# Attention and FFN kernel: two score chunks ahead of the transposes in steps 0 and 1, no clearing of y, bias first in a batch's first steps, the last block transfers issued by two engines

## What is computed

```python
x = L0_attn_x                          # (2, 1024, 512), float32
xn = _layernorm(x, axis=-1)
s = _L0_attn_ref(xn, ...)
g = _silu(_L0_ffn_ref(xn, ...))
x = x + s * g
```

## Time and profile before

| | us |
|---|---|
| median of 3 runs | 2310.16 |
| the runs | 2310.16, 2304.26, 2310.84 |
| the profiled execution, whole | 2305.63 |
| its span from first to last instruction | 2303.8 |
| busy: PE, DVE, ACT, POOL | 2193.3, 1806.7, 1330.2, 792.2 |
| mean granted TensorE clock | 0.989 of full speed |

### The profile page before, as it was taken

One profiled execution on the slowest core, in us unless ns is written; L12 is line 12 of the kernel. 1 busy time (PEld: TensorE's weight loads), 2 busy tenths in 40 slices (PEclk: granted clock), 3 DMA queues, 4 the chain that ended last, 5 costly groups with the idle time before them and its releaser, 6 DMA issues.

```text
span 2303.8 us, 37079 instructions
## 1 busy us (share of the span) xinstructions
PE 2193.3 (95%) x10928; PEld 1845.2 (80%) x10928; DVE 1806.7 (78%) x3917; ACT 1330.2 (58%) x3700; POOL 792.2 (34%) x2053
## 2 busy tenths in 40 slices
PE   5999999999999999799989999999999999998998
PEld 5888888888888888588877888878888878876887
DVE  5889899999989989723369898989898989896132
ACT  3666666666666666433356666666666666654333
POOL 1424242424242424144514242424242424221443
PEclk8999999999999999999999999999999999999999
DMA  2454556454545454623325555555545555445223
GB/s 97 128 122 122 128 123 126 126 127 125 124 123 128 124 127 123 164 83 133 119 77 127 126 125 127 123 124 126 128 122 127 124 128 122 101 122 137 96 96 110
DMA packets 432682, 278.93 MB, mean 121 GB/s; under 512 B 55520, under 2 KB 416096, under 8 KB 428512
## 3 DMA queue, kind: packets, MB, share of 16 engines
q1 hardware_dynamic: 432480, 276.56, 48.0%
HBM read 119.12 MB, written 6.29 MB: 54 GB/s over the span
## 4 chain that ended last, share of the span: by engine, by line
PE 85%; DVE 5%; issue 4%; SPq 2%; POOL 2%; ACT 2%; DMA 1%; DVEq 0%; ACTq 0%; POOLq 0%
PE out_ps L425 17%; PE out_ps L437 14%; PE score_ps L411 10%; PE even_ps L388 7%; PE qkv_ps L388 6%; PE third_ps L411 5%; PE score_ps L499 5%; PE qkv_ps L499 5%; PE even_ps L389 3%; PE qkv_ps L389 3%; PE even_ps L515 3%; SPq L306 2%; DVE probs L831 1%; PE third_ps L515 1%; PE out_ps L515 1%
## 5 line engine op out<-in xcount | busy, mean ns | idle before, releaser
L845 DVE TENSOR_TENSOR pT_lo<-pT_lo,pT_hi 128x512 fp32r<-128x512 f32 x576 | 380.1, 704 | 95.1 <-ACT pT_hi L595 95.0
L587 ACT ACTIVATE probs<-probs,low_min 128x896 f32<-128x896 f32 (+7 forms) x512 | 394.9, 780 | 97.4 <-DVE low_min L820 95.6
L595 ACT ACTIVATE pT_hi<-pT_lo 128x512 fp32r<-128x512 f32 x576 | 330.7, 622 | 173.5 <-PE out_ps L425 119.9
L831 DVE STREAM_TRANSPOSE probs<-probs 128x896 f32<-128x896 f32 (+7 forms) x512 | 373.9, 753 | 0.7
L1045 POOL TENSOR_SCALAR rs_x<-sq_sum 128x5 f32<-128x5 f32 x122 | 33.6, 275 | 901.2 <-ACT natural L563 898.6
L425 PE MATMUL out_ps<-pT_hi,kv_hi 128*128 128x512 f32 x576 | 236.6, 411 | 50.0 <-issue 45.8
L600 ACT ACTIVATE attT_hi<-att 128x512 fp32r<-128x512 f32 x128 | 81.0, 632 | 328.6 <-DVE att L852 328.6
L425 PE MATMUL out_ps<-pT_hi,kv_lo 128*128 128x512 f32 x576 | 225.9, 392 | 0.0
L425 PE MATMUL out_ps<-pT_lo,kv_hi 128*128 128x512 f32 x576 | 225.5, 392 | 0.0
L437 PE MATMUL out_ps<-o_hi,attT_hi 128*128 128x512 f32 x512 | 213.1, 416 | 9.3 <-DVE attT_lo L859 9.3
L820 DVE CUSTOM_DVE_ANT_0 probs<-score_ps,rel_sb,slope 128x384 f32<-128x384 f32 (+5 forms) x352 | 203.7, 589 | 1.9 <-PE score_ps L411 1.1
(11 more groups left out here) (203 smaller groups left out, 6052.1 us busy)
## 6 DMA issues: line engine op xcount, KB each, us to landing
qkv_raw<-w_ffn_dram SPq DMA_DIRECT2D x44, 768.0 KB, 4.3
att<-rec_out_at SPq DMA_DIRECT2D x128, 256.0 KB, 5.1
pT_lo<-probs SPq DMA_DIRECT2D x256, 128.0 KB, 3.6
pT_lo<-probs SPq DMA_DIRECT2D x256, 112.0 KB, 3.6
pT_lo<-probs SPq DMA_DIRECT2D x256, 96.0 KB, 3.1
qkv_raw<-w_qkv_dram SPq DMA_DIRECT2D x15, 1536.0 KB, 6.5
pT_lo<-probs SPq DMA_DIRECT2D x256, 80.0 KB, 2.6
o_raw<-w_o_dram SPq DMA_DIRECT2D x16, 1024.0 KB, 5.5
```

The costliest lines, as they stand in the source:

```text
L587: act.activation(row, row, ACT.Exp, scale=-1.0, bias=low_min[:, i % 2, h, HEAD_CHUNKS[i] - 1:HEAD_CHUNKS[i]], accum_out=row_sum[:, i % 2, ...
L595: act.activation(pT_hi[:, (U * TURNS + n) % HIGH_SLOTS, :], home(i, j).bitcast(F32), ACT.Copy).then_inc(probs_high, 1)
L831: dve.transpose(row, row).then_inc(probs_turned, 1)
L845: dve.tensor_tensor(out=home(i, j), in0=home(i, j).bitcast(F32), in1=pT_hi[:, (U * TURNS + n) % HIGH_SLOTS, :].bitcast(F32), op=ALU.subtra ...
```

## The change

It does four things; the matmuls and the transfers are the same.

1. `parts_of` returns `SBANKS - (i < LAG)` for `between`: in steps 0 and 1 of every unit but a batch's first, two chunks of `scores` (and two `bias`) stand between `project` and `turn_qk`, not three. The third follows `out_project` (on VectorE `add_y`). These are 14 units with two such steps each.
2. The clearing of `y` is gone with its semaphore. In the second unit of a batch steps 0 to 2 copy into `y` in place of adding.
3. In steps 0 and 1 of a batch's first unit VectorE runs all four `bias` before `low_q` and `low_k`. In step 0 `early_norms` of the third tile moves from before the `bias` to behind `low_k`; in the first batch the two `low_x` of that step move ahead of `low_q`.
4. In the last step 7 of each batch SyncE issues 8 of the 16 transfers. The other 8 are issued by ScalarE in step 8, behind `high_att` and before `high_probs`.

```diff
-            return (SBANKS, 2 * SBANKS, chunks) if i >= HT else (0, SBANKS, chunks)
+            return (SBANKS, 2 * SBANKS, chunks) if i >= HT else (0, SBANKS - (i < LAG), chunks)
...
                     for k in range(BLOCKS):
-                        to, what = block_of(i, a, (a + k) % BLOCKS)
-                        sp.dma_start(to, what).then_inc(probs_back[t % 2], 16)
+                        if not (last and i == TILES - 1 and k >= BLOCKS // 2):
+                            to, what = block_of(i, a, (a + k) % BLOCKS)
+                            sp.dma_start(to, what).then_inc(probs_back[t % 2], 16)
...
+            def send_last_probs(U):
+                t = tile(U, TILES - 1)
+                act.wait_ge(probs_turned, t * G)
+                act.wait_ge(weighed, homes_free(U, TILES - 1))
+                for a in range(BLOCKS):
+                    for k in range(BLOCKS // 2, BLOCKS):
+                        to, what = block_of(TILES - 1, a, (a + k) % BLOCKS)
+                        act.dma_start(to, what).then_inc(probs_back[t % 2], 16)
...
                         high_att(U, i)
+                    if i == TILES:
+                        send_last_probs(U)
...
-                    if first and i == 0:
-                        early_norms(tile(U, 2))
...
+                    if first and i < LAG:
+                        between = chunks
                     for k in range(ahead, between):
                         bias(U, i, k)
+                    if first and i == 0 and U == 0:
+                        for t in range(HT, HT + 2):
+                            low_x(0, t)
...
                             dve.wait_ge(y_free, b + 1)
-                            dve.memset(y[:, TILES - LAG - 1:TILES, :], 0.0).then_inc(y_zero, 1)
-                            dve.wait_ge(y_zero, b + 1)
-                        add_y(U, i, first)
+                        add_y(U, i, first or U % UNITS == 1 and i <= LAG)
                     for k in range(between, chunks):
                         bias(U, i, k)
-                    if first and i == 0 and U == 0:
-                        for t in range(HT, HT + 2):
-                            low_x(0, t)
+                    if first and i == 0:
+                        early_norms(tile(U, 2))
```

More of the change, by code:

```diff
@@ L141, in build @@
         xn_done, xT_turned, xT_high, xT_low = sem("xn_done"), sem("xT_turned"), sem("xT_high"), sem("xT_low")
-        y_free, y_zero = sem("y_free"), sem("y_zero")
+        y_free = sem("y_free")
         w_high, w_split, o_high = sem("w_high"), sem("w_split"), sem("o_high")
@@ L293, in rec_home, with turn_probs @@
                              ).then_inc(rec_back[slot], 16)
-            def turn_probs(U, i, first):
+            def turn_probs(U, i, first, last):
                 t = tile(U, i)
@@ L335, in attention @@
                         rec_away(U, i)
-                        turn_probs(U, i, first)
+                        turn_probs(U, i, first, last)
                         if last and i == TILES - 1:
```

## The result

| | before | after |
|---|---|---|
| median of the runs made side by side, us | 2307.61 (11 runs) | 2315.59 (11 runs) |
| lowest and highest | 2304.26, 2310.84 | 2312.24, 2319.40 |
| span of the profiled execution | 2303.8 | 2315.1 |

The changed kernel takes 1.0037 times as long, with a 95% interval of 1.0029 to 1.0045: +8.5 us (+6.7 to +10.4). The estimate is 0.37%, and the interval begins at 0.29%. The prediction was +2.0 us, with "no difference" within 0.3% as the likeliest; the kernel is slower by four times that. The time itself lies inside the range of 2303 to 2322.

The account below looks back on a forecast made before the run. The prediction took TensorE, busy 95% of the span, as the bound, so only its gaps matter. Terms +1.65 - 2.7 - 1.9 - 0.1 + 5.0 = +2.0 us on 2307.9 gave 2310 us, range 2303 to 2322.

Parts of the forecast that it names:

- its term of the sum, +5.0 us: Last unit's step 8: eight ScalarE issues at 0.65 us delay `weigh` of tile 6 by 2.07 and 2.91 us.
- the low clock behind the longer gap: Step 8: a longer TensorE gap may bring the low clock; counted only in the chance of slower, no size given.
- the cover: Step 8: VectorE's idle wait for `out_project` before `add_y`, 3.13 and 2.29 us, hides part of the issues' delay.
- Rival C: Step 8 of the last units: both issuing engines hold each other up, alternating; +15.4 there, total +12.4, 2320 us; chance 0.20.
- Part 1 was predicted +1.65: Step 1: the copy `pT_hi` behind the fourth exponential decides; 11 of 14 steps end 0.15 us later, +1.65 us.
- Part 2, -2.7: Step 3 of each batch's first unit: no clear saves 1.6 us; second batch gives 0.5 back to SyncE's issue queue.
- Part 3, -0.1 and -1.9: Batch starts: first batch -0.1 us, gain against tile 4's later projection; second -1.9 us, as SyncE's issues start earlier.
- s: The gain of the first batch's step 0 from the new order, between 0 and 3.2 us, taken as 1.65.
- its own rule: The prediction called itself wrong in sign with issues under 0.3 us, in size with issues over 1 us.

Follow-up runs that it names:

- part 3 alone: The kernel before with only the bias-first order in steps 0 and 1 of a batch's first unit: 0.9997 (0.9988 to 1.0005), -0.7 us.
- the kernel of part 1: The kernel before with only two chunks of scores between project and turn_qk in steps 0 and 1: 1.0003 (0.9994 to 1.0013), +0.7 us.

## Why the prediction was wrong

**Part 4 is the step that failed: its term of the sum, +5.0 us, is mis-sized.** The run with it alone says +14.8. The prediction took the length of a ScalarE issue from SyncE's rows, 0.65 us, and put the low clock behind the longer gap at nothing in the sum. The mechanism was right: the eight issues stand ahead of `pT_hi`, and the cover is the wait of `add_y` for `out_project`. Three numbers tell where the 10 us come from.

- The length of an issue: 0.65 us was taken from SyncE's rows, at a time when only one engine issues. It was 1.08 while both did. Over two batches that is 16 x 0.43 = 6.9 us. The run with SyncE silent and the one with 16 KB transfers, both at 0.64 us, show that the 0.65 was right for what it was measured at, and wrong for here. That the latter gave +4.9 us in all, the predicted term, is in part luck: by its trace 3.7 are the later `weigh` of tile 6 and the rest the low clock.
- The low clock behind the longer gap. The prediction names it as a thing that may come, and puts it into a chance, not into the sum. By the next `weigh` it cost 1.6 us a batch in the changed kernel, 3.3 in all.
- The cover was right. The copies started 8.82 us behind the start of `high_att` (963.53 and 954.71) and not 0.53 (956.90 and 956.37 in the kernel before), a delay of 8.29 us; TensorE's gap grew from 0.83 to 6.10, by 5.27. The difference is 3.02, where 3.13 was said.

5.0 + 6.9 + 3.3 is 15.2, with 14.8 measured (11.5 to 17.8). The traces of the two kernels, laid over each other, give 10.9 for the two `weigh` of tile 6 and 3.3 behind them, 14.2.

**Rival C had the size and not the reason.** It gave +15.4 for this part, and said that the engines alternate. They do not: with small transfers both issue at 0.64 us at once, and with large ones both start at 0.6 to 0.7. Its price, 1.3 us an issue, was too high by 3.5 us in all, and the clock's 3.3, which it did not have, made up for it: its size was luck. What could have told the reason ahead is a product: 128 KB each 0.65 us (the 5.23 us for eight of the kernel before, above) is 200 GB/s, and the window of the kernel before with a DMA share of 1.00, shown above, has 218. A second engine that issues can't add what the DMA engines don't have. The prediction read the issue as a cost of the sequencer and never multiplied bytes by rate.

**Part 1 was predicted +1.65 and measured +0.7 (-1.4 to +3.0).** The mechanism is seen in the rows, the copy that waits for the fourth exponential. In unit 2, counted from the end of `out_project`, `weigh` starts 0.18 us earlier (0.13 was predicted) and the copy 0.12 later (0.15). But the last tile comes only 0.01 later and not 0.15, because VectorE's first two `pT_lo` take 1.29 us together and no longer 1.39. The order of the waits was right; the term was too large, since most of the copy's delay is made up before the last tile. The rows of all 14 steps give +0.7, and no timed run can tell that from nothing.

**Part 2, -2.7, measured -2.1 (-4.2 to -0.2).** The gap of the first batch went from 3.10 to 1.39 us as said (to "about 1.5"), and 2.0 us stay, where 1.6 were predicted. For the second batch the prediction let 0.5 us be given back to the issue queue; against the profiled execution all 1.7 were. What the edit saves there, it saves where the low clock would have followed the gap, which was not foreseen. So the sum is right, in part by luck.

**Part 3, -0.1 and -1.9.** The second batch: -1.9 for SyncE's issues, right; by the trace of part 3 alone 1.4 of it arrive at the later `weigh`. The first: the loss at tile 4's projection was put at between +1.6 and -1.6 us with s = 1.65, and came out at about +0.5 in the changed kernel; s was smaller than the loss, about 1.0 where 1.65 was taken. The bounds of the prediction had it inside. Part 3 alone measured -0.7 us (-2.8 to +1.2) in all.

**The sum.** Parts 1 to 3 were -3.0 and measured -5.3 (-7.4 to -3.2); part 4 was +5.0 and measured +14.8; the whole +2.0 and measured +8.5. By its own rule (over 1 us an issue, wrong in size) it named the case in which it would fail, and gave it 0.20. The evidence against that case, the 0.60 us in the median of 2048 issues, was all from stretches in which a single engine issued. It was not quite steady either: 43 of the 2048 took more than 0.9 us, and what held them up stays open.

## What to carry to other kernels

Before a second engine is given issues of a stream of transfers, multiply the size of one by the rate of issue: if one engine alone comes near what the DMA engines move, the second gains nothing, and both pay with longer issues that hold up whatever stands behind them. Put issues behind the instruction that somebody waits for, not ahead of it. A gap on TensorE of 3 us or more mostly cost more than itself here, since matmuls at half speed followed it (once behind 1.88 us too). Shortening such a gap can be worth more than the gap; or nothing, where the next step waits for transfers anyway, as in the second batch.

## What the runs showed of the hardware

- ScalarE's issue, alone, costs what SyncE's does (0.64 us in the median of 16, 0.60 for SyncE), and it runs beside ScalarE's own earlier arithmetic: the issue at 957.91 starts while the copy of `att` begun at 957.50 is still running, and three more lie beside the `pT_hi` copies. Only what stands behind the issues waits.
- Two engines issued at 0.64 us each at the same time with 16 KB transfers (DMA share 0.27), and at 1.08 and 1.22 us with 128 KB (share 0.92 at 193 GB/s); the first two or three of each engine's took 0.6 to 0.72 us with 128 KB too.
- Behind gaps of 3.60 and 3.57 us at the same place, the kernel of part 1 went to the low clock and the kernel before did not (1219 and 1220 us above). Such stretches were worth 1.5 to 2.7 us each. That executions of one kernel differ in it too is seen in the granted clock of the runs: of 23 executions of the kernel before in one session, 2302.20 to 2312.38 us long, the four at 0.986 took 2309.6 us in the mean, and the three at 0.990 or more 2304.1. A single profiled execution is one of these.
